# The last norm of a graph kernel in two equal halves: four one-column powers, one matmul moved behind the first transposes, two stores in place of three

## The reference

```python
h = relu(A @ (x @ W1) + b1);  h = relu(A @ (h @ W2) + b2)
x = layernorm(x + h)
y = (A @ x @ V1 + A @ A @ x @ V2 + A @ A @ A @ x @ V3) / 3
out = layernorm(x + y)      # over the 128 features of each row, eps 1e-5
```

## Time and profile before

| what | us |
|---|---|
| median of 3 runs (lowest to highest) | 256.37 (255.79 to 256.46) |
| the profiled execution, its own time | 256.48 |
| its span, first to last instruction | 254.7 |
| the last matmul of the hops starts | 246.79 |
| the last store is issued | 252.13 |

### The profile page before, as it was taken

One profiled execution on the slowest core, in us unless ns is written; L12 is line 12 of the kernel. 1 busy time (PEld: TensorE's weight loads), 2 busy tenths in 40 slices (PEclk: granted clock), 3 DMA queues, 4 the chain that ended last, 5 costly groups with the idle time before them and its releaser, 6 DMA issues.

```text
span 254.7 us, 3758 instructions
## 1 busy us (share of the span) xinstructions
PE 247.2 (97%) x1152; PEld 204.3 (80%) x1152; DVE 200.9 (79%) x391; ACT 193.1 (76%) x337; POOL 16.7 (7%) x24
## 2 busy tenths in 40 slices
PE   8999999999999999999999999999999999999991
PEld 8688788888888888877888888888888888888880
DVE  0898899796789889898778777767676767888844
ACT  2897998886868787978877787867677776788751
POOL 1000000000003021130000000000000000303032
PEclk9999999999999999999999999999999999999999
DMA  6999999920000000000000000000000000010111
GB/s 213 389 386 385 387 386 387 400 91 0 0 3 3 0 0 3 0 0 1 0 4 0 0 0 3 0 0 1 4 0 0 0 3 0 0 42 0 45 41 42
DMA packets 11396, 20.49 MB, mean 80 GB/s; under 512 B 1264, under 2 KB 2288, under 8 KB 11248
## 3 DMA queue, kind: packets, MB, share of 16 engines
q1 hardware_dynamic: 11088, 19.93, 21.4%
q10 hardware_dynamic: 288, 0.33, 0.4%
HBM read 19.20 MB, written 1.05 MB: 80 GB/s over the span
## 4 chain that ended last, share of the span: by engine, by line
PE 82%; SPq 5%; DMA 4%; DVE 3%; ACT 2%; issue 2%; POOL 0%; POOLq 0%; DVEq 0%; ACTq 0%
PE filters L393 17%; PE filters L386 17%; PE filters L387 17%; PE pair L393 9%; PE pair L386 9%; PE pair L387 9%; DMA adj<-a_t 4%; SPq L271 3%; PE weighted L361 2%; PE turned L363 2%; ACT ring_high L517 2%; DVE ring_low L632 1%; SPq L269 1%; SPq L275 1%; DVE operand_low L586 1%
## 5 line engine op out<-in xcount | busy, mean ns | idle before, releaser
L632 DVE TENSOR_TENSOR ring_low<-adj,ring_high 128x512 fp32r<-128x512 f32 x240 | 160.0, 688 | 34.8 <-ACT ring_high L517 32.0
L517 ACT ACTIVATE ring_high<-adj 128x512 fp32r<-128x512 f32 x240 | 148.6, 629 | 32.7 <-PE filters L387 15.9
L386 PE MATMUL filters<-ring_high,operand_low 128*128 128x512 f32 x156 | 62.0, 398 | 0.0
L393 PE MATMUL filters<-ring_low,operand_high 128*128 128x512 f32 x156 | 61.2, 392 | 0.4 <-DVE ring_low L632 0.4
L387 PE MATMUL filters<-ring_high,operand_high 128*128 128x512 f32 x156 | 60.8, 390 | 0.0
L393 PEld LDWEIGHTS filters<-ring_low,operand_high 128*128 128x128 f32 x156 | 29.3, 188 | 8.0 <-DVE ring_low L632 1.8
L387 PEld LDWEIGHTS filters<-ring_high,operand_high 128*128 128x128 f32 x156 | 29.3, 188 | 5.7
L386 PEld LDWEIGHTS filters<-ring_high,operand_low 128*128 128x128 f32 x156 | 29.3, 188 | 5.7
L386 PE MATMUL pair<-ring_high,operand_low 128*128 128x512 f32 x84 | 33.3, 396 | 0.0
L393 PE MATMUL pair<-ring_low,operand_high 128*128 128x512 f32 x84 | 33.1, 394 | 0.2
L387 PE MATMUL pair<-ring_high,operand_high 128*128 128x512 f32 x84 | 32.7, 390 | 0.0
(11 more groups left out here) (84 smaller groups left out, 209.0 us busy)
## 6 DMA issues: line engine op xcount, KB each, us to landing
adj<-a_t SPq DMA_DIRECT2D x48, 256.0 KB, 9.6
resident_raw<-a_t SPq DMA_DIRECT2D x16, 256.0 KB, 9.7
nodes<-x_rows SPq DMA_DIRECT2D x1, 1024.0 KB, 11.6
lead<-lead_in SPq DMA_DIRECT2D x3, 256.0 KB, 4.7
out_rows<-nodes SPq DMA_DIRECT2D x3, 256.0 KB, 2.4
lead<-lead_in ACTq DMA_DIRECT2D x1, 192.0 KB, 2.9
lead<-lead_in SPq DMA_DIRECT2D x1, 128.0 KB, 2.7
lift_raw<-lifts SPq DMA_DIRECT2D x1, 128.0 KB, 11.3
```

Source lines behind the costliest of these rows:

```text
L386: nc.tensor.matmul(bank, y_low, a_high, start=first, stop=False)
L393: used = nc.tensor.matmul(bank, y_high, a_low, start=False, stop=last)
L517: nc.scalar.activation(ring_high[:, n % RING, :], source, ACT.Copy).then_inc(high_ready, 1)
L632: nc.vector.tensor_tensor(ring_low[:, n % RING, :], source, ring_high[:, n % RING, :].bitcast(F32), ALU.subtract).then_inc(low_ready, 1)
```

## The change

The last chunk is handled in halves, two tiles and two tiles. The first half's residual (256 columns) and that of the third tile stay ahead of the transposes; the fourth tile's residual goes behind the first two. The first half and the second half each take two bn_stats, two bn_aggr and one addition of eps, through the functions that the other norms use. POOL takes four powers of one column each. The shift and ACT's two applications go; DVE applies all four tiles, each as its rstd is there. SP stores the first half after two of them, ACT the second half after four.

```diff
-PIECES = (slice(0, 2), slice(2, 3), slice(3, 4))
...
+        last_banks = [weighted[:, 0, :], weighted[:, 1, :], turned[:, 0, :], pair[:, 0, 0:D]]
...
-            for piece in range(1, len(PIECES)):
-                tiles = last_tiles(piece)
-                sp.wait_ge(last_normalised, piece)
-                sp.dma_start(out_rows[:, tiles, :], nodes[:, tiles, :]).then_inc(out_stored, 16)
-
-            sp.wait_ge(out_stored, 16 * (CHUNKS - 1 + len(PIECES)))
+            sp.wait_ge(last_normalised, half_tiles)
+            sp.dma_start(out_rows[:, last_tiles(0), :], nodes[:, last_tiles(0), :]).then_inc(out_stored, 16)
+
+            sp.wait_ge(out_stored, 16 * (CHUNKS - 1 + HALVES))
...
-            for piece, part in enumerate(PIECES):
-                pool.wait_ge(variance_ready, whole_groups * HALVES + piece + 1)
-                nc.gpsimd.tensor_tensor(rstd[:, part], variance[:, part], exponent[:, part], ALU.pow
-                                        ).then_inc(rstd_ready, 1)
+            for half, part in enumerate(halves):
+                pool.wait_ge(variance_ready, whole_groups * HALVES + half + 1)
+                for t in range(part.start, part.stop):
+                    nc.gpsimd.tensor_tensor(rstd[:, t:t + 1], variance[:, t:t + 1], exponent[:, t:t + 1], ALU.pow
+                                            ).then_inc(rstd_ready, 1)
...
-            for piece in range(len(PIECES)):
-                nc.tensor.matmul(piece_bank(piece), ident[:], nodes[:, last_tiles(piece), :], start=True, stop=False)
-            for piece, part in enumerate(PIECES):
-                pe.wait_ge(chunk_evacuated, HOPS * CHUNKS + part.start // half_tiles)
-                for t in range(part.start, part.stop):
-                    last = nc.tensor.matmul(piece_bank(piece)[:, t - part.start, :], chunk_t[:, t * P:(t + 1) * P],
-                                            ident[:], start=False, stop=(t == part.stop - 1))
-                last.then_inc(post_multiplied, 1)
+
+            def add_sums(t):
+                return nc.tensor.matmul(last_banks[t], chunk_t[:, t * P:(t + 1) * P], ident[:], start=False, stop=t > 0)
+
+            first_half = nodes[:, last_tiles(0), :]
+            nc.tensor.matmul(weighted[:, 0:half_tiles, :], ident[:], first_half, start=True, stop=False)
+            nc.tensor.matmul(last_banks[2], ident[:], nodes[:, TILES - 2, :], start=True, stop=False)
+            pe.wait_ge(chunk_evacuated, HOPS * CHUNKS)
+            add_sums(0)
+            add_sums(1).then_inc(post_multiplied, 1)
+            nc.tensor.matmul(last_banks[3], ident[:], nodes[:, TILES - 1, :], start=True, stop=False)
+            pe.wait_ge(chunk_evacuated, HOPS * CHUNKS + 1)
+            add_sums(2)
+            add_sums(3).then_inc(post_multiplied, 1)
...
-            act.wait_ge(shift_ready, whole_groups * HALVES + 1)
-            for t in range(half_tiles):
-                nc.scalar.activation(nodes[:, TILES - TPC + t, :], weighted[:, t, :], ACT.Identity, bias=shift[:, t:t + 1],
-                                     scale=rstd[:, t:t + 1]).then_inc(normalised, 1)
-            tiles = last_tiles(0)
-            act.wait_ge(normalised, whole_groups * TPC + half_tiles)
-            act.dma_start(out_rows[:, tiles, :], nodes[:, tiles, :]).then_inc(out_stored, 16)
+            act.wait_ge(last_normalised, TPC)
+            act.dma_start(out_rows[:, last_tiles(1), :], nodes[:, last_tiles(1), :]).then_inc(out_stored, 16)
...
-            done = HOPS * CHUNKS - 1
-            for piece, part in enumerate(PIECES):
-                m = whole_groups * HALVES + piece
-                dve.wait_ge(post_multiplied, done + piece + 1)
-                for t in range(part.start, part.stop):
-                    last = nc.vector.bn_stats(stats[:, t, :], piece_bank(piece)[:, t - part.start, :])
-                last.then_inc(stats_ready, 1)
...
-            norm_shift(HOPS - 1, CHUNKS - 1, 0)
-            for piece in range(1, len(PIECES)):
-                t = PIECES[piece].start
-                dve.wait_ge(rstd_ready, whole_groups * HALVES + piece + 1)
-                nc.vector.tensor_scalar(nodes[:, TILES - TPC + t, :], piece_bank(piece)[:, 0, :], moments[:, t, 0:1],
-                                        rstd[:, t:t + 1], ALU.subtract, ALU.mult).then_inc(last_normalised, 1)
+            hop, c = HOPS - 1, CHUNKS - 1
+            for half in range(HALVES):
+                dve.wait_ge(post_multiplied, HOPS * CHUNKS + half)
+                norm_stats(hop, c, half, last_banks[halves[half]])
+                norm_moments(hop, c, half)
+            for t in range(TPC):
+                dve.wait_ge(rstd_ready, whole_groups * HALVES + t + 1)
+                nc.vector.tensor_scalar(nodes[:, TILES - TPC + t, :], last_banks[t],
+                                        moments[:, t, 0:1], rstd[:, t:t + 1], ALU.subtract, ALU.mult
+                                        ).then_inc(last_normalised, 1)
```

More of the change, by code:

```diff
@@ L232, in residuals, with last_tiles @@
             return NORMED.index(hop) * CHUNKS + c + 1
[L234 to L242, removed]
+        def last_tiles(half):
+            return slice(TILES - TPC + half * half_tiles, TILES - TPC + (half + 1) * half_tiles)
+        last_banks = [weighted[:, 0, :], weighted[:, 1, :], turned[:, 0, :], pair[:, 0, 0:D]]
         def half_of(hop, c, half):
@@ L552, in norm_stats @@
                 for t in range(half_tiles):
-                    last = nc.vector.bn_stats(stats[:, half * half_tiles + t, :], rows[:, t, :])
+                    last = nc.vector.bn_stats(stats[:, half * half_tiles + t, :], rows[t])
                 last.then_inc(stats_ready, 1)
@@ L605, in visits @@
                         dve.wait_ge(residual_added, residuals(hop, c))
-                        norm_stats(hop, c, half, nodes[:, first:first + half_tiles, :])
+                        norm_stats(hop, c, half, [nodes[:, first + t, :] for t in range(half_tiles)])
                     for hop, c in norms(n, "moments", half):
```

## The result

| what | before | after |
|---|---|---|
| median of 8 runs each, us | 256.34 (255.79 to 256.46) | 255.62 (255.08 to 255.74) |
| ratio, 95% interval | | 0.9971 (0.9960 to 0.9983) |
| the profiled execution, us | 256.48, span 254.7 | 255.64, span 253.8 |

The prediction was 256.3 with a range of 255.8 to 256.9. The measured 255.62 is 0.72 under before and just outside the range. By the text's bound of 0.3% it is the edge between "same" and "faster"; a ratio of 1 lies outside the interval.

A forecast was written before the change was run, and what follows sets the result against it. PE's matmuls, busy 247.2 of 254.7 us, bound the kernel, so only the tail could change: -0.13 PE, +0.24 POOL and -0.20 store make -0.09, from the median 256.37 to 256.28, say 256.3 us; range 255.8 to 256.9.

The forecast's parts named there:

- Part 1: PE in the tail: without the pair residual ahead, the first transpose's weights load 0.13 us earlier; bounds 0 and 0.22.
- Part 2: DVE's tail statistics: 1.19 us from first bn_stats to first power, as before; a gain of 0.5 if POOL can use it.
- Part 3: POOL's tail powers: four of 0.55 us in steps of 0.51; the last ends 0.11 later, and POOL sets the end.
- Part 4: DVE's four tail applications: 0.41 us each, DVE keeps up; taking away the shift and ACT's applications gives nothing by itself.
- Part 5: Last store, 128 KB from ACT's queue: lands in 2.0 us against 2.2, gain 0.2; application's end to issue stays 0.10.
- Rival 1: POOL's tail powers: single ones follow no closer than 0.64 us; +0.3, 256.7 us; chance 0.20.
- Rival 2: POOL's tail powers: stretched by DVE's work beside them to 0.87 us each; 257.6 us; chance 0.06.
- Rival 3: DVE's variance and POOL's power in the tail exclude each other; +0.26, 256.6 us; chance 0.08.
- Rival 4: The change helps: powers nearer the lowest step, store at 1.7 to 1.9; -0.3 to -0.8, 255.6 to 256.1 us; chance 0.10.

The follow-up runs named there:

- r4_long_warm: The changed kernel with 40 warming matmuls in place of 7; ratio to before 1.0283, median 263.48 us.
- r2_wait_order: The kernel before with two of DVE's waits in the tail exchanged, its own statistics first, then the earlier norm's shift; ratio to before 0.9997.
- r1_pow_pairs: The changed kernel with one power of two columns for each half in place of four of one; ratio to before 0.9981, median 255.72 us.
- r3_pow_pairs: The changed kernel with one power of two columns for each half, repeated in a later set; ratio to before 0.9975.
- r3_pieces_rest: The kernel before with the fourth residual moved behind two transposes, two DVE waits exchanged and one SP store of 128 KB; ratio to before 0.9971.
- r3_two_stores: The kernel before with SP's two stores of 64 KB made one of 128 KB, issued when both tiles are normalised; ratio to before 1.0003.
- r4_same_before: The kernel before again with no edit, as the null of its set; ratio to before 0.9993.

## Why the prediction was wrong, point by point

**The step that failed** is the one from the tail's sum to the median: "On the median: 256.28", with "the runs' spread" of three runs as its only allowance. I let the time ahead of 247 us stand as fixed. It isn't: up to the mark it varied by 0.9 us over seventeen profiles of the same code, and a set's mean moved by 0.4 against what the tails say. In the four later sets the ratio is 0.9998, 0.9990, 0.9990 and 0.9988, and the difference of the means +0.12, -0.21, -0.19 and -0.25 us. The tails, five after (7.58, 7.77, 7.65, 7.57, 7.67, mean 7.65) against three before (7.91, 7.92, 8.08, mean 7.97), say -0.32; with the executions' own times less M in place of the spans (mean 9.47 against 9.75) it is -0.28. r4_long_warm is not among the five; with its 9.65 it would be -0.25. So some 0.4 of the first set's 0.72 isn't the change's. That it was a draw fits the marks (35.85 and 35.30 in the two profiles of the first set); nothing in the first set's timed runs can show it, since only their spans are known.

**The sum itself was a third of the true one**, -0.09 against -0.28 to -0.32. A gain of this size alone would have ended at some 256.0 to 256.1, inside the range. Its terms:

| term | predicted | measured |
|---|---|---|
| moved residual, to the first bn_stats | -0.13 | -0.14 |
| order of DVE's waits, to the first power | 0 | -0.07 |
| four powers in place of three | +0.24 | +0.23 (2.07 against 1.84) |
| from application's end to issue | 0 | -0.07 |
| landing of the last store | -0.20 | -0.22 (mean 1.98 against 2.2) |

The measured terms add up to -0.27, in agreement with the -0.28; the tails' -0.32 carries the rounding of the spans. Two terms that the prediction put at nothing, the order of the waits and the time from end to issue, make half of it.

- Part 1 was right to 0.01: the weights load at 247.09, 0.05 after ACT's end at 246.66 + 0.38. The wait on ACT took 0.09 of the 0.22, as worked out.
- Part 2 said "the first half takes the same" 1.19. It takes 1.13, because the shared function waits for the statistics first and for the old shift second. r2_wait_order shows that this is worth 0.07 at the first power and 0.20 at the last application, over three pieces. The diff had it; I read the function for what it computes and not for the order of its waits.
- Part 3 was right: steps of 0.51, and POOL sets the end. The powers take back more than the moved residual gives. r1_pow_pairs and r3_pow_pairs show it from the other side: 0.18 less at the application.
- Part 4 was right in its size, 0.41 each, and in that DVE keeps up.
- Part 5 had the landing right in size, and its reason (the small store ran behind the other) fits the runs; its allowance of 0.10 from end to issue was SP's queue, which the changed kernel's last store doesn't meet. The last store landed in 2.1 to 2.5 in all seven profiles that had ACT's 128 KB issued 0.14 to 0.37 before it, whether it was of 64 or of 128 KB. It landed in 1.8 to 2.1 in the other eleven, where the one ahead was 0.87 us or more away, or was of 64 KB and 0.32 or 0.50 away. The groups touch at 2.1, and no run moves one store against the other with all else the same, so the size of the effect is rough. In the changed kernel there are 1.0 us between the stores, because DVE applies both halves in turn.
- Rival 1 fell (steps of 0.50 to 0.52). Rival 2 fell (0.54 to 0.56 each, beside DVE's applications). Rival 3 fell: the second half's variance at 249.53 ran inside the power of 249.48 to 250.04, at its usual 0.17. The Trainium skill (SBUF — State Buffer, Who interferes with whom) names tensor_scalar among the operations that can contend with GpSimd; on these two columns the trace shows no such wait. Rival 4 came nearest in size, but not by its terms: the powers' step and the landing are those of the forecast.

**The best versions** are r1_pow_pairs / r3_pow_pairs (0.9981 and 0.9975) and r3_pieces_rest (0.9971). The two were not told apart; by tails the first is 0.2 shorter (7.43 and 7.44 against 7.63), and the tail of r3_pieces_rest, 0.3 under the kernel before, accounts for 0.9987 and not for 0.9971; the rest is of the size of the first set's. Both beat the kernel before; against the changed kernel of its set r3_pow_pairs is 0.43 lower in the median (255.55 against 255.98), of which the tails show 0.13 (7.44 against 7.57).

## What to carry to other kernels

Split the span at a mark that no edit touches before believing a difference of 0.3%: a set of 8 runs moved by 0.4 us, and what differed between profiles was the start, where loads land and the first matmuls speed up sooner or later. In a tail of single instructions, read a diff also for the order of its waits and for how many stores one queue issues; each was worth 0.07 us or more here, half of the moved matmul. And keep the last store clear of a large one ahead: where only 0.14 to 0.37 us lay between them it landed up to 0.5 us later, and two tails with earlier applications ended no sooner.

## What the runs showed of the hardware

SP issued its two stores of 64 KB 0.71 to 0.73 us apart in all five profiles that have them (the fifth is r4_same_before, 251.25 and 251.96), though an issue shows 0.33. In r2_wait_order the second tile was ready 0.24 before its issue, and with the first store taken away (r3_two_stores) the issue came 0.03 after the application: both speak for a limit of SP's queue. Two waits of DVE ahead of bn_aggr, one for its own last result and one long fulfilled, cost 0.07 us more when the fulfilled one is written first (0.60 against 0.53 in r2_wait_order). PE's first matmuls, 14 to 28 records, ran at about half the rate of those behind them (421 against 275 ns each, starts 0.21 against 0.11 us apart), with a granted clock of 1.00 on either side; the change came anywhere from 4.2 to 7.2 us.
